# One kernel for a two-layer gated stack: the second attention with stationary values in column tiles, and biases in fewer products

## The reference, cut to what matters

```python
# B: query = layernorm(x), key = value = ctx_1024 (120 rows a sequence); D_K = 16, 16 heads
Q = (query @ Wq + bq).reshape(B, Tq, NUM_HEADS, D_K).transpose(0, 2, 1, 3)
K = (key @ Wk + bk).reshape(B, Tk, NUM_HEADS, D_K).transpose(0, 2, 1, 3)
V = (value @ Wv + bv).reshape(B, Tk, NUM_HEADS, D_K).transpose(0, 2, 1, 3)
scores = jnp.einsum('bhtd,bhsd->bhts', Q, K) / jnp.sqrt(jnp.float32(D_K))
attn = jax.nn.softmax(scores, axis=-1)
ctx = jnp.einsum('bhts,bhsd->bhtd', attn, V)
return ctx.transpose(0, 2, 1, 3).reshape(B, Tq, D_MODEL) @ Wo + bo
# the router
logits = xt @ Wr + br
pr, idx = jax.lax.top_k(logits, 2)
```

## Time and profile before

| | us |
|---|---|
| median of 3 runs | 1848.67 (1848.36 to 1865.61) |
| the profiled execution: its time | 1838.81 |
| the profiled execution: its span | 1837.2 |
| first part: first to last `B.q` on ACT (16 batches) | 222.7 to 1133.0 |
| second part, from about | 1220 |

### The profile page before, as it was taken

One profiled execution on the slowest core, in us unless ns is written; L12 is line 12 of the kernel. 1 busy time (PEld: TensorE's weight loads), 2 busy tenths in 40 slices (PEclk: granted clock), 3 DMA queues, 4 the chain that ended last, 5 costly groups with the idle time before them and its releaser, 6 DMA issues.

```text
span 1837.2 us, 35831 instructions
## 1 busy us (share of the span) xinstructions
PE 1540.0 (84%) x12221; PEld 1239.6 (67%) x12222; DVE 1121.2 (61%) x2782; ACT 886.8 (48%) x2169; POOL 591.9 (32%) x704
## 2 busy tenths in 40 slices
PE   2334899999998999899989877649999999999994
PEld 1223577667766767676766554438888888888884
DVE  4657678877787778787777552234444444444442
ACT  1111466656666656665655453214444544445542
POOL 0002324333434243334332421023443434434432
PEclk9557999999999999999999896569999999999998
DMA  5002211222022202221122000157213232232224
GB/s 172 11 0 78 81 57 37 92 92 84 10 92 92 91 9 87 92 93 43 51 84 84 7 7 12 48 160 239 39 32 100 34 103 34 33 101 34 29 34 114
DMA packets 63088, 123.60 MB, mean 67 GB/s; under 512 B 13890, under 2 KB 51899, under 8 KB 58811
## 3 DMA queue, kind: packets, MB, share of 16 engines
q1 hardware_dynamic: 45675, 102.75, 16.3%
q0 software_dynamic: 17312, 19.56, 6.6%
HBM read 78.63 MB, written 48.04 MB: 69 GB/s over the span
## 4 chain that ended last, share of the span: by engine, by line
PE 76%; DVE 9%; ACT 7%; issue 3%; DMA 2%; POOL 1%; SPq 0%; ACTq 0%; DVEq 0%; POOLq 0%
PE bank L1247 17%; PE bank L1249 16%; PE bank L1248 16%; PE bank L1319 9%; PE bank L1343 7%; PE bank L1332 3%; ACT b_ex L687 2%; DVE b_mn L1008 2%; ACT b_q L747 1%; PE bank L1359 1%; PE bank L1521 1%; ACT r_z L670 1%; PE bank L1467 1%; PE bank L1411 1%; PE bank L1431 1%
## 5 line engine op out<-in xcount | busy, mean ns | idle before, releaser
L1247 PE MATMUL bank<-split_room,wm 128*128 128x256 f16 x1152 | 314.9, 273 | 8.3 <-issue 6.9
L1249 PE MATMUL bank<-split_room,wm 128*128 128x256 f16 x1152 | 314.8, 273 | 0.0
L1248 PE MATMUL bank<-split_room,wm 128*128 128x256 f16 x1152 | 314.7, 273 | 0.0
L1224 DVE SCALAR_TENSOR_TENSOR split_room<-bank,b12e,split_room 128x256 f32<-128x256 f32 x288 | 138.3, 484 | 266.0 <-ACT split_room L798 258.2
L798 ACT ACTIVATE split_room<-bank,b12e 128x256 f32<-128x256 f32 x288 | 134.3, 470 | 196.0 <-PE bank L1249 192.6
L687 ACT ACTIVATE b_ex<-bank,b_mn 128x120 f32<-128x120 f32 x512 | 143.6, 373 | 117.5 <-DVE b_mn L1008 116.4
L1319 PE MATMUL bank<-b_k,b_q 128*128 128x480 f32 x256 | 140.8, 634 | 39.0 <-ACT b_ex L687 23.3
L1343 PEld LDWEIGHTS bank<-b_v,b_pt 120*128 120x128 f32 x1024 | 137.9, 204 | 36.0 <-issue 31.7
L643 POOL DMA_INDIRECT acc<-split_room,m_cur x72 | 115.3, 1602 | 131.7 <-ACT split_room L812 104.3
L1247 PE MATMUL bank<-wm,split_room 128*128 128x256 f16 x576 | 157.0, 273 | 0.0
L1249 PE MATMUL bank<-wm,split_room 128*128 128x256 f16 x576 | 157.0, 273 | 0.0
(11 more groups left out here) (358 smaller groups left out, 3859.7 us busy)
## 6 DMA issues: line engine op xcount, KB each, us to landing
split_room<-in_L_ffn_W SPq DMA_DIRECT2D x48, 512.0 KB, 8.4
wsplit<-split_room SPq DMA_DIRECT2D x16, 1536.0 KB, 6.5
wm<-wsplit SPq DMA_DIRECT2D x16, 1536.0 KB, 8.9
acc<-x SPq DMA_DIRECT2D x17, 256.0 KB, 2.1
xin<-in_x SPq DMA_DIRECT2D x16, 256.0 KB
rows<-r_row SPq DMA_DIRECT2D x16, 256.0 KB, 8.2
ct<-in_ctx SPq DMA_DIRECT2D x16, 120.0 KB
cb<-in_ctx SPq DMA_DIRECT2D x16, 120.0 KB, 2.1
```

Source lines behind the costliest of these rows:

```text
L1224: dve.scalar_tensor_tensor(m_h[:, c % 3], bank[c % 4][:, TILE:2 * TILE], b12e[:, p, 1, c:c + 1], m_s[:, c % 2], ALU.add, ALU.mult).then_in ...
L1247: pe.matmul(o, lh, rh, start=start, stop=False)
L1248: pe.matmul(o, ll, rh, start=False, stop=False)
L1249: return pe.matmul(o, lh, rl, start=False, stop=stop)
```

## The change

The `B.p` rounds are turned round. The values of a head become the stationary operand, 32 columns wide (16 of them are zero), and the transposed exponents stream, 128 columns. The four heads of a round write to the four groups of 32 partitions of the bank, so each of the four products uses another quarter of the array's columns. Rounds r of one t add up in the bank (`start=r == 0`, `stop=r == per - 1`): each has its 16 values in another place of the 32 (`head_of` tells which head stands where). The result is thereby already transposed, and `B.ot` goes.

The sums no longer come from a column of ones: each exponent instruction on ACT also gives the sum of its row (`accum_out`). DVE takes the reciprocals (`B.rx`), spreads each over 16 columns (`b_rx`), PE transposes that tile behind the last values (two transposes for each t), ACT copies it to `b_z` (`B.r3`, `B.r7`), DVE multiplies the values with it (`B.p3`, `B.p7`), ACT makes the high half (`B.o0`, `B.o1`) and DVE the low one. All that is done for each t by itself, and `B.out` waits for one t at a time, behind the bias.

The biases: high and low halves now stand in rows 0 and 32 of one operand of 33 rows, so `B.k` and `B.out` have one bias product where they had two. `br` is added by DVE where it copied the logits before, and its products go. The load of the biases has 8 more small DMAs on SP, once.

All lists in `ORDER` are new.

```diff
+HL = 33
+VHALF = H1 // 2 * PITCH + K1
...
-        ones_h = sb("ones_h", [1, P], f16)
+        ones_h = sb("ones_h", [HL, P], f16)
...
-        bk_h = sb("bk_h", [1, 2, H1 * PITCH], f16)
+        bk_h = sb("bk_h", [HL, H1 * PITCH], f16)
...
-        b_v = sb("b_v", [S, H1, K1 + 1])
+        b_v = sb("b_v", [S, 2 * VHALF])
+        b_vd = b_v[:, :].rearrange("s (a m) -> s a m", a=2)[:, :, 0:H1 // 2 * PITCH].rearrange("s a (n d) -> s a n d", d=PITCH)
...
+        b_sum = sb("b_sum", [P, NT, H1])
...
+        b_rx = sb("b_rx", [P, NK, P])
...
+        def head_of(r, j):
+
+            return 8 * (r % 2) + 2 * j + r // 2
...
-            "PE": ("F.ht1/2 A.s0/0 B.t3/3 B.s4/3 B.p2/3 A.s1/0 A.t0/0 B.s5/3 B.t4/3 F.d0/2 B.s6/3 B.p3/3 F.d1/2 B.p4/3 "
-                "B.t5/3 B.s7/3 A.t1/0 A.p0/0 B.t6/3 B.p5/3 A.p1/0 B.t7/3 F.t/1 B.p6/3 B.p7/3 A.ot/0 B.ot/3 F.gu0/1 "
...
+            "PE": ("A.s0/0 F.ht1/2 B.t2/3 B.s3/3 B.p1/3 A.s1/0 A.t0/0 B.t3/3 B.s4/3 B.p2/3 F.d0/2 B.s5/3 B.t4/3 B.s6/3 "
+                "B.p3/3 F.d1/2 B.p4/3 A.t1/0 B.t5/3 B.s7/3 A.p0/0 B.t6/3 B.p5/3 A.p1/0 F.t/1 B.t7/3 A.ot/0 B.p6/3 B.p7/3 "
...
+                        if G is B and (not isinstance(b, int) or b >= 1):
+                            act.wait_ge(B.rd, (b - 1) * NT + k // per + 1)
...
-                            last = act.activation(ex[:, k % 2, h], sb_[:, h * S:(h + 1) * S], ACT.Exp,
-                                                  bias=mn[:, k % 2, h:h + 1], scale=-1.0)
+                            at = head_of(k % per, h)
+                            last = act.activation(ex[:, k % 2, h], sb_[:, h * S:(h + 1) * S], ACT.Exp, bias=mn[:, k % 2, h:h + 1], scale=-1.0,
+                                                  accum_out=b_sum[:, k // per, at:at + 1] if G is B else None)
...
+            def b_r_(t):
+                def stage(b, p):
+                    held(act, B.pv_mm, b * NT + t + 1)
+                    act.activation(b_o[:, t], bank[5][:, D:2 * D], ACT.Copy).then_inc(B.rt, 1)
+                return stage
+
+            def b_o_(t):
+                def stage(b, p):
+                    held(act, B.o, b * NT + t + 1)
+                    act.activation(b_ot[:, 0, :, t * P:(t + 1) * P], b_o[:, t].rearrange("p (k q) -> p k q", k=NK), ACT.Copy).then_inc(B.ot_hi, 1)
                 return stage
...
+                if G is A:
+                    made.update({f"{G.name}.p{k}": values(k) for k in range(per - 1, n, per)})
...
+            def b_rx_(t):
+                def stage(b, p):
+                    dve.wait_ge(B.exp, b * RB + (t + 1) * (RB // NT))
+                    dve.reciprocal(b_rd[:, t], b_sum[:, t]).then_inc(B.rd, 1)
+                    if t or not isinstance(b, int) or b >= 1:
+                        held(dve, B.pv_mm, b * NT + t)
+                    dve.wait_ge(B.rd, b * NT + t + 1)
+                    dve.tensor_copy(b_rx[:, :, :].rearrange("p k (h d) -> p (k h) d", d=K1), over(b_rd[:, t], K1)).then_inc(B.rx, 1)
...
+            def b_p_(t):
+                def stage(b, p):
+                    dve.wait_ge(B.rt, b * NT + t + 1)
+                    dve.tensor_tensor(b_o[:, t], bank[5][:, 0:D], b_o[:, t], ALU.mult).then_inc(B.o, 1)
+                return stage
+
+            def b_o_(t):
+                def stage(b, p):
+                    dve.wait_ge(B.ot_hi, b * NT + t + 1)
+                    c = slice(t * P, (t + 1) * P)
+                    dve.tensor_tensor(b_ot[:, 1, :, c], b_o[:, t].rearrange("p (k q) -> p k q", k=NK), b_ot[:, 0, :, c], ALU.subtract).then_inc(B.ot, 1)
+                return stage
...
-                cr.link(dve.tensor_copy(r_lg[:, :, :], bank[5][:, 0:NT * NE].rearrange("p (t e) -> p t e", t=NT)))
+                dve.wait_ge(misc_in, 64)
+                cr.link(dve.tensor_tensor(r_lg[:, :, :], bank[5][:, 0:NT * NE].rearrange("p (t e) -> p t e", t=NT),
+                                          br_s[:, :].unsqueeze(1).to_broadcast([P, NT, NE]), ALU.add))
...
-                        for h in range(h0, h0 + QUAD):
-                            last = pe.matmul(pbk[:, h * (width + 1):(h + 1) * (width + 1)], pt[:, k % 2, h - h0],
-                                             v[:, h] if G is B else v[:, :], start=True, stop=True)
+                        if G is A:
+                            for h in range(h0, h0 + QUAD):
+                                last = pe.matmul(pbk[:, h * (width + 1):(h + 1) * (width + 1)], pt[:, k % 2, h - h0],
+                                                 v[:, :], start=True, stop=True)
+                        else:
+                            r, c = k % per, k % per % 2
+                            for j in range(QUAD):
+                                at = r // 2 * (H1 // 2 * PITCH) + (4 * c + j) * PITCH
+                                last = pe.matmul(pbk[PITCH * j:PITCH * (j + 1), c * P:(c + 1) * P], v[:, at:at + PITCH], pt[:, k % 2, j],
+                                                 start=r == 0, stop=r == per - 1)
+                            if r == per - 1:
+                                pe.wait_ge(B.rx, b * NT + t + 1)
+                                for i in range(NK):
+                                    last = pe.transpose(pbk[:, D + i * P:D + (i + 1) * P], b_rx[:, i], ident)
...
-                    pe.wait_ge(G.ot, b + 1)
+                    if G is A:
+                        pe.wait_ge(G.ot, b + 1)
                     for t in range(NT):
                         o, c = bk[:, t * D:(t + 1) * D], slice(t * P, (t + 1) * P)
                         if bias is not None:
-                            pe.matmul(o, ones_h[:, :], bias[:, 0], start=True, stop=False)
-                            pe.matmul(o, ones_h[:, :], bias[:, 1], start=False, stop=False)
+                            pe.matmul(o, ones_h[:, :], bias[:, :], start=True, stop=False)
+                            pe.wait_ge(G.ot, b * NT + t + 1)
...
-                    for i in range(2):
-                        pe.matmul(bank[4][:, c * S:(c + 1) * S], bk_h[:, i, c * P:(c + 1) * P], ones_h[:, 0:S], start=i == 0, stop=False)
+                    pe.matmul(bank[4][:, c * S:(c + 1) * S], bk_h[:, c * P:(c + 1) * P], ones_h[:, 0:S], start=True, stop=False)
...
-                    pe.matmul(o, ones_f[:, :], br_s[:, :], start=True, stop=False)
                     for k in range(NK):
-                        last = pe.matmul(o, r_zt[:, k, t * P:(t + 1) * P], wr_s[:, k], start=False, stop=k == NK - 1)
+                        last = pe.matmul(o, r_zt[:, k, t * P:(t + 1) * P], wr_s[:, k], start=k == 0, stop=k == NK - 1)
```

More of the change, by code:

```diff
@@ L1022, in rounds @@
                 made = by_round(G, n, s=minima)
[L1023 to L1024 removed]
+                if G is A:
+                    made.update({f"{G.name}.p{k}": values(k) for k in range(per - 1, n, per)})
+                return made
+            def b_rx_(t):
[11 more added lines that the diff above has]
+                    dve.tensor_tensor(b_o[:, t], bank[5][:, 0:D], b_o[:, t], ALU.mult).then_inc(B.o, 1)
+                return stage
+            def b_o_(t):
[3 more added lines that the diff above has]
+                    dve.tensor_tensor(b_ot[:, 1, :, c], b_o[:, t].rearrange("p (k q) -> p k q", k=NK), b_ot[:, 0, :, c], ALU.subtract).then_inc(B.ot, 1)
+                return stage
             ra = rounds(A, RA, bank[0], bank[2], a_mn, a_rd, a_o, H0, K0)
```

68 lines of the change are left out of this document (38 added, 30 removed), and 8 rows, old and new, of the table ORDER.

## The result

The changed kernel takes 1892.4 us (median of 4 runs, 1885 to 1896), the kernel before 1848.5 beside it (4 runs): a ratio of 1.026, 95% interval 1.019 to 1.033. It is slower by some 44 us. I had said 1838, and 1798 to 1878. The sets are e1 to e4, e5 to e8, e9 to e12, e13 to e16, and e17 with e18, each on a chip of its own, and the first pair. Kernels of one set compare directly; across sets a difference of chips can be in it. A trace is of one execution.

The account below looks back on a forecast made before the run. PE was taken as the bound, its work plus its waits: biases -1.3, values -1.3, waits +1.7, so -0.9 us a batch, -14 for 16. With +6 and -2 at the ends, about -11: 1838 on the median, range 1798 to 1878.

Parts of the forecast that it names:

- Net +1.7 for the waits: PE's waits in one batch: 3.9 us added less 2.2 us removed, net +1.7 us.
- Biases, -1.3 us a batch: Bias products in `B.k` (0.25), `B.out` (0.24) and the router (0.83) dropped from PE's work: -1.3 us a batch.
- I count both: A period is PE's work plus its waits, so changes in both are summed and multiplied by 16 batches.
- Values, -1.3: Value products of the eight rounds: only neighbouring quarters overlap, 0.72 us a round, -0.14 each, -1.3 us a batch.
- my first rival: Value products: all four quarters run at once, saving 3.9 us a batch instead of 1.3; 1802 us, chance 0.24.
- the 3 that I had named as a sign of being wrong: The forecast is wrong if PE's work in a period falls by more than 3 us.
- The sums, +0.4 a round: ACT's exponents that also give sums: 0.1 us more a head, 0.4 a round, felt at rounds 1 and 2.
- Waits removed, -2.2: PE's waits at the end of B (0.60 + 0.41, falling to 0.1) and the 1.28 go: -2.2 us a batch.
- The 1.28: PE's transposes waiting for the copy of the ones before; goes, as `A.s0` and `F.ht1` stand between rounds 1 and 2.
- 0.60 + 0.41 ahead of `B.out`: PE's waits at `B.ot` for DVE and at `B.out` for DVE's low half; to fall to 0.1 together.
- Waits added, +3.9: New waits on PE: round 1 0.4, round 2 0.4, round 6's scores 2.2, transposes of the reciprocals 0.9 us a batch.
- ScalarE as the bound (1867): Between rounds 0 and 7 a sum costs 0.2 us, not 0.1, adding 1.6 a batch; 1867 us, chance 0.16.

Follow-up runs that it names:

- e1: The changed kernel with two entries of VectorE's list moved back behind the minima that they hold up (`A.rot`, `F.q1c`): 1931 us, ratio 1.043.
- e4: The changed kernel with its stages in the order of the four lists of before, the pieces of `B.ot` put in: 1886 us, ratio 1.017.
- e5: The changed kernel, new order, without accumulator output: PE makes the sums by a second product with a block of ones: 1863 us, ratio 1.018.
- e8: The kernel before with the bias edits alone: 1832 us, ratio 1.001.
- e9: The changed kernel with 13 transposes that nobody reads on PE ahead of the scores of round 6: 1868 us, ratio 1.014.
- e12: The kernel before with unread transposes on PE, 5 ahead of the scores and 9 ahead of the transposes of round 2: 1823 us, ratio 0.986.
- e13: e11 with 8 more unread transposes ahead of R's transposes: 1805 us beside 1826 for the kernel before, ratio 0.989.
- e16: e6 with unread transposes in four of PE's waits: 1821 us, ratio 0.997.
- e17: The kernel before with unread transposes in three waits, as e13 but without the bias edits: 1820 us beside 1824, ratio 0.996.
- e18: e13 with one entry of VectorE's list moved, `F.gu2` ahead of `F.q0a`: 1838 us, ratio 1.008.
- e11: e8 with unread transposes on PE, 4 ahead of the scores and 9 ahead of the transposes of round 2: 1823 us, ratio 0.986.
- e3: The changed kernel without the exponents' sums (no accumulator output, sums stand at 1.0): 1857 us, ratio 1.004.
- e7: e4 without the exponents' sums (no accumulator output, sums stand at 1.0): 1829 us beside 1830 for the kernel before, ratio 1.000.
- e14: The changed kernel with unread transposes in three waits: 14 ahead of round 2's scores, 13 ahead of round 6's, 8 ahead of R's transposes: 1849 us, ratio 1.012.
- e15: e3 with the same unread transposes in three waits as e14: 1853 us, ratio 1.014.
- e6: e5 in the order of the lists before: 1826 us, ratio 0.996.
- e10: e6 with six entries of the PE and VectorE lists moved, for the waits of its trace: 1894 us, ratio 1.023.

## Why the prediction was wrong

Two steps failed. *Net +1.7 for the waits* is what turned the sign: at full clock PE's work fell by 3.8 us a period and its idle time rose by 6.2 (5.0 to 11.3), so that the period grew from 59.8 to 62.2 with no help from the clock. *The clock*, which has no term in the sum, about doubled that: 64.5 on average, for 60.1.

- *Biases, -1.3 us a batch.* Right in size (router 0.95 for 0.9; e8's periods 58.7 for 59.8). Wrong in the step from work to time: "I count both", PE's work plus its waits, held the clock for given, and the other waits too: in e11 and e13 most of the saving became idle time.
- *Values, -1.3.* Mis-sized, in the good direction: 0.45 a round, not 0.72. All four quarters run at once, my first rival's mechanism; PE's work fell by 3.8 in all, not 2.6, by more than the 3 that I had named as a sign of being wrong. The Trainium skill, "TensorE: Matmul & The Clock Gate", Part 3, which the prediction cites, gives tiles in different places of the array the length of one product and about 4 ns for each further one, and the trace agrees: eight products in 0.36 us, a change of form included, where one after the other would be 0.88. The rival's time, 1802, was still far off: it was the right mechanism with the wrong bound.
- *The sums, +0.4 a round.* The duration was right: 1.47 us for four, +0.36. Felt at rounds 1, 2 and 6 and at the ends it made 25 us in my sum (3 x 0.4 x 16, and 6). Less the experts' extra work e3 gives some 51 us for it, and e4 against e7 some 2.6%, 47 us: twice my term. With the waits filled it is 12 (e14, e15). So the step from an instruction's cost to the kernel's gave half of what it is, and with the waits filled most of the cost is gone.
- *Waits removed, -2.2.* The 1.28 went. Of the 0.60 + 0.41 ahead of `B.out` I left 0.1; it is 1.09. DVE's low half ends at about 722.8, so the chain behind the last values is longer than PE's cover; both had come out at 3.1 us in my sum, with no margin either way.
- *Waits added, +3.9.* Round 6 1.91 for 2.2, the reciprocals 0.88 for 0.9: right. Round 2 has 1.97 in all for my 1.2, and three were missed: 0.35 (round 1), 0.49 (`A.s0` for `A.rot`), 0.36 (A's second values). I had read the new order of PE's list and not asked what DVE's list puts ahead of each minima; from the scores of round 1 to those of round 2 it is 4.13 us (681.47 to 685.60) where I had a turn of 3.46. What the new order costs in all depends on the rest: 37 us in e5 against e6, 3 to 21 in the other traces.
- *The clock: not in the sum at all.* At full clock the changed kernel has periods of 61.8 and 62.2, 2.0 to 2.4 over before; with it pulled down 64.9. e9 gives back 1.2% by useless work alone. The rival that came nearest, ScalarE as the bound (1867), is not what happened: an exponent's sum cost 0.1, as in the forecast, and not its 0.2.

What is shown: without the read-outs the loss is gone (e3), and fillers in one wait give back nearly half of it (e9, 1.2 of 2.6%). What is not: how much of the sums' cost goes through the clock and how much through longer waits (e15 has less low time than e3 and no shorter periods), how much of the loss is the new order, and what holds e10's reciprocal.

## What to carry to other kernels

Saving work on the engine that bounds a kernel counts only if its idle time does not grow with it: before you believe such a saving, look for what else ends each of its waits, list by list. And where the profile has a row for the granted clock, a bound engine that idles more may run slower as well: compare periods with the clock at 1.00 first, then the others. A test costs one kernel: fill the waits with products that nobody reads. It gave 1.2 to 1.4% where low pieces of the clock cost time (e9, e12), 0.4% where the kernel had few (e17), and nothing in e15 and e16.

And when an experiment leaves out a result that later parts depend on, compare the later parts first: here the experts had 152 products and 16 us more, which hid a third of what the sums cost.

## What the hardware showed that I had not expected

- A read-out of the accumulator on ScalarE is an instruction of its own, 0.20 us, which half overlaps: an exponent of 120 columns follows its forerunner after 0.35 instead of 0.25 us or so (four in 1.47 for 1.11).
- TensorE's clock fell to 1.2 GHz behind waits of 1.97 us and of 1.91 and 0.88, for 6.8 and 3.4 us, in most periods of the changed kernel; but in e8 also 0.4 us behind a wait of 1.28 (12.7 us into the period), in a period whose twin, with the same waits, kept 2.4 GHz. With 13 transposes in the waits there those pieces went (e11).
- VectorE's product of 512 columns from and to the on-chip memory (SBUF) took 1.57 us in the changed kernel, beside GpSimd's product of 1.38 us (from 685.20) and the start of its block of 3.55 (from 686.56). One from a bank took 0.68 just ahead (683.86), beside another product of GpSimd. In the kernel before, the same instruction has no work of GpSimd beside it; one pair of places shows this, and no run tests it (timeline, DVE):

```profile
655.92 0.68 DVE L994 TENSOR_TENSOR a_t<-a_t,a_z 128x512 f32<-128x512 f32 x1
```

- A reciprocal of 256 columns takes VectorE 1.74 us, a product of as many 0.42.
